# Graph network kernel: histogram products without the weights, weight sums by a segment scan, coefficient rows read ahead of four gather chunks

## The reference

```python
# layer 0: attention, one softmax per target over its edges
e = leaky_relu(concat([h[src], h[dst], emb_rel[etype]]) @ attn_w1 @ attn_w2, 0.01)
a = softmax of e over the edges of each dst
x = x + relu(where(deg > 0, segment_sum(a * h[src], dst), h) + h @ loop_weight)
# layer 1: plain sums over source nodes
x = x + relu(concat([h, segment_sum(h[dst] @ W_msg + b_msg, src)]) @ W_upd + b_upd)
# layer 2: two rounds with edge weights w
norm = maximum(segment_sum(w, dst), 1.0) ** -0.5
h = segment_sum((h * norm)[src] * w, dst) * norm        # twice; mean of the three h
# layer 3: attention with 8 heads and self loops, then a two-layer net with layer norms
```

## Time and profile before

| what | us |
|---|---|
| runs | 3965.01, 3946.61, 3963.30 (median 3963.3) |
| the profiled execution | 3954.3 |
| its span, first to last instruction | 3952.6 |
| PE busy | 2834.4 |
| VectorE busy | 2382.7 |
| POOL busy | 1904.0 |
| ScalarE busy | 480.0 |
| mean granted clock | 0.64 |

### The profile page before, as it was taken

The page is one execution under the profiler, slowest core; times in us unless marked ns, Lnnn a source line. Parts: engine busy times, 40 slices in busy tenths (PEclk is TensorE's granted clock), DMA queues, the critical chain, the costliest instruction groups (busy, mean ns, idle before and its releaser), DMA issues.

```text
span 3952.6 us, 46035 instructions
## 1 busy us (share of the span) xinstructions
PE 2834.4 (72%) x14097; PEld 2257.3 (57%) x14098; DVE 2382.7 (60%) x4263; ACT 480.0 (12%) x934; POOL 1904.0 (48%) x1767
## 2 busy tenths in 40 slices
PE   1984688788888499979979947777300226999894
PEld 1981111577777399979923336666300006999873
DVE  5678999777777688830010069999708463555433
ACT  0000000233323000014400012222100011000011
POOL 1778777767777200000000047777078787777200
PEclk9555555555555555559989969999755555555575
DMA  2314455387887622205466801111021134244100
GB/s 88 122 48 103 110 141 144 96 191 184 198 183 185 175 78 81 62 17 183 157 259 255 296 27 50 52 52 51 35 67 42 53 124 134 84 117 118 32 1 8
DMA packets 244087, 434.92 MB, mean 110 GB/s; under 512 B 137949, under 2 KB 139847, under 8 KB 230391
## 3 DMA queue, kind: packets, MB, share of 16 engines
q10 hardware_dynamic: 126289, 182.23, 16.6%
q1 hardware_dynamic: 60614, 190.34, 13.1%
q0 software_dynamic: 57056, 60.74, 8.3%
HBM read 276.41 MB, written 156.60 MB: 110 GB/s over the span
## 4 chain that ended last, share of the span: by engine, by line
PE 50%; DVE 18%; POOL 13%; issue 10%; DMA 6%; DVEq 1%; ACT 1%; ACTq 1%; SPq 0%; POOLq 0%
POOL ring L620 10%; PE PS L975 9%; PE PS L1180 7%; PE PS L1080 6%; PE PS L1082 5%; PE PS L1013 4%; PE PS L1151 4%; PE PS L1215 3%; DVE big L1921 3%; DMA qa<-d_code 3%; DMA arena<-d_code 2%; PE PS L1262 2%; PE PS L1159 2%; PE PS L1205 2%; DVE big L1915 2%
## 5 line engine op out<-in xcount | busy, mean ns | idle before, releaser
L620 POOL DMA_INDIRECT ring<-d_h,idx_lin x1568 | 1675.3, 1068 | 1581.7 <-DMA d_h<-Hn 1038.4
L1080 PE MATMUL PS<-qa 128*125 128x150 bf16 x1050 | 414.4, 395 | 105.8 <-DVE arena L1654 46.1
L1262 PEld LDWEIGHTS PS<-arena,s_ring 128*128 128x128 f32 x1968 | 438.4, 331 | 9.8 <-issue 1.3
L1262 PE MATMUL PS<-arena,s_ring 128*128 x1968 | 432.4, 414 | 0.0
L1082 PE MATMUL PS<-qa 128*125 128x150 bf16 x1050 | 401.1, 382 | 0.0
L975 PEld LDWEIGHTS PS<-arena,s_ring 128*125 128x125 f32 x1632 | 342.8, 332 | 0.4 <-issue 0.4
L975 PE MATMUL PS<-arena,s_ring 128*125 x1632 | 342.8, 416 | 0.0
L1080 PEld LDWEIGHTS PS<-qa 128*125 128x125 bf16 x1050 | 262.6, 250 | 135.9 <-DVE qa L1647 95.9
L1847 DVE TENSOR_SCALAR s_ring<-iota_row,arena 128x125 f32<-128x125 f32 x816 | 280.4, 346 | 77.7 <-ACT arena L719 19.8
L1180 PE MATMUL PS<-big,arena 125*64 125x500 f32 (+1 forms) x700 | 268.7, 546 | 25.7 <-DVEq L1315 25.7
L1082 PEld LDWEIGHTS PS<-qa 128*125 128x125 bf16 x1050 | 264.3, 252 | 0.0
(11 more groups left out here) (441 smaller groups left out, 4068.0 us busy)
## 6 DMA issues: line engine op xcount, KB each, us to landing
big<-d_wgt SPq DMA_DIRECT2D x50, 1562.5 KB, 7.4
d_stash<-ring SPq DMA_DIRECT2D x196, 256.0 KB
arena<-d_stash ACTq DMA_DIRECT2D x196, 256.0 KB, 2.7
big<-d_cnt SPq DMA_DIRECT2D x25, 1562.5 KB, 6.5
ring<-d_h,idx_lin POOLq DMA_INDIRECT x1568
d_cnt<-big ACTq DMA_DIRECT2D x13, 1562.5 KB
d_wgt<-big ACTq DMA_DIRECT2D x13, 1562.5 KB
d_cnt<-arena ACTq DMA_DIRECT2D x12, 1562.5 KB
```

Of the source, the lines that this page charges most:

```text
L620: pool.indirect_dma_start(ring[:, HALF * h + s, :], None, table, bass.IndirectOffsetOnAxis(ap=idx_lin[:, CH * i + s:CH * i + s + 1], axis= ...
L1080: nc.tensor.matmul(bank(3 * half + s // 2, NP, 2 * CW, at), lhs, hot_step(half, s, W, 2 * CW), start=(s % 2 == 0), stop=False, skip_group_ ...
L1262: mm = nc.tensor.matmul(PS[:, bass.ds(place[s] + j % SUMS * BANK, D)], marks[:, j % 2, s, :], arena[:, bass.ds(at[s], D)], start=False, st ...
```

## The change

- The histogram multiplies the counts' one-hot alone: the moving operand has 25 columns instead of 100. L1447, `w3` with its five preparing instructions, and the reduction into `norm` (L1474) go.
- The edge weights are written to memory (`d_wl`) beside the other edge tables, and read back to `w_edge` before the softmax ends. Behind `softmax0`, VectorE clears `norm` and runs one `scan_one` over them, which gives a running sum per target (`w_sum`); PE gets one more `chain` for it. SP writes it to `d_wsum`, and POOL reads the sum at each target's last edge into `norm` with 25 indirect transfers.
- SP's stash loop stops before chunk 94 (`ALPHA_AT`): there it issues the load of `w_edge`, waits for the coefficients and writes them. POOL stops before the same chunk, waits for that write, reads the coefficient rows and only then gathers chunks 94 to 97. `d_wsum` and the first count blocks follow on SP behind the rest of the stash loop.
- Wait counts of later semaphore uses are raised accordingly.

```diff
-        h_bf = s_flat[:, RING * W // 2:RING * W // 2 + RING * 4 * HW // 2].bitcast(BF16)
+        h_bf = s_flat[:, RING * W // 2:RING * W // 2 + RING * HW // 2].bitcast(BF16)
...
@@ sync
             sp.dma_start(d_dst.rearrange("(p c) k -> p (c k)", p=P), junk[:, 0:C]).then_inc(S["dst_out"], 16)
+            sp.dma_start(d_wl.rearrange("(p c) k -> p (c k)", p=P), w_lin).then_inc(S["dense_out"], 16)
...
                         sp.dma_start(fa0, d_fa0.rearrange("(p c) k -> p (c k)", p=P)).then_inc(S["fill_in"], 16)
+                    if turn == 0 and i == ALPHA_AT:
+                        sp.wait_ge(S["blk_ready"], NB)
+                        sp.wait_ge(S["dense_out"], 32)
+                        sp.wait_ge(S["fill_in"], 16)
+                        sp.dma_start(w_edge, d_wl.rearrange("(p c) k -> p (c k)", p=P)).then_inc(S["fill_in"], 16)
+                        sp.wait_ge(S["alpha_ready"], 1)
+                        sp.dma_start(d_al0.rearrange("(p c) k -> p (c k)", p=P), qa[:, 0:C]).then_inc(S["alpha_out"], 16)
                     sp.wait_ge(S[f"stash_got{h}"], CH * 16 * stash_turns(turn, i))
...
             stash(0)
 
-            sp.wait_ge(S["alpha_ready"], 1)
-            sp.dma_start(d_al0.rearrange("(p c) k -> p (c k)", p=P), qa[:, 0:C]).then_inc(S["alpha_out"], 16)
-
             sp.wait_ge(S["blk_out0"], 32 * (NB // 2 + 2))
             sp.wait_ge(S["blk_out1"], 32 * (NB // 2 + 1))
             sp.wait_ge(S["alpha_out"], 16)
+            sp.wait_ge(S["alpha_ready"], 2)
+            sp.dma_start(d_wsum.rearrange("(p c) k -> p (c k)", p=P), w_sum).then_inc(S["alpha_out"], 16)
             sp.wait_ge(S["steps_in"], 32)
...
@@ gpsimd
             block_rows(d_dst, dstl, "drow0_in")
-            tiles(0, d_h0, 40, NCH)
+            tiles(0, d_h0, 40, ALPHA_AT)
             pool.wait_ge(S["alpha_out"], 16)
             block_rows(d_al0, alpha0, "rows_in")
+            tiles(0, d_h0, ALPHA_AT, NCH)
...
+            pool.wait_ge(S["alpha_out"], 32)
+            for b in range(NB):
+                pool.indirect_dma_start(norm[:, b:b + 1], None, d_wsum, bass.IndirectOffsetOnAxis(ap=last_i[:, b:b + 1], axis=0),
+                                        bounds_check=EP - 1, oob_is_err=False).then_inc(S["nodes_in"], 16)
...
@@ tensor
-                mm = nc.tensor.matmul(bank(7, NP, 4 * NB), free(s_bf[:, 0:1], [[HALF, NP]], h * W * HALF + s_),
-                                      free(h_bf[:, 0:1], [[HW * HALF, 4], [HALF, NB]], h * 4 * HW * HALF + s_),
+                mm = nc.tensor.matmul(bank(7, NP, NB), free(s_bf[:, 0:1], [[HALF, NP]], h * W * HALF + s_),
+                                      free(h_bf[:, 0:1], [[HALF, NB]], h * HW * HALF + s_),
                                       start=(c == 0), stop=(c == C - 1))
...
             chain(1)
             chain(1, 1)
+            chain(1)
             pe.wait_ge(S["rows_in"], 16 * KG)
...
@@ vector
-            for j in range(3):
-                go(v_.tensor_copy(w3[:, j, :], w_lin))
-                if j < 2:
-                    go(v_.tensor_tensor(w_lin, w_lin, w3[:, j, :], ALU.subtract))
...
-                go(v_.tensor_tensor(hot_d, iota_d[:, 0:HW, :], dhi_at[:, :, c:c + HALF], ALU.is_equal))
-                v_.tensor_tensor(free(h_bf[:, 0:1], [[HW * HALF, 3], [HALF, HW], [1, HALF]], (h * 4 + 1) * HW * HALF),
-                                 free(h_bf[:, 0:1], [[0, 3], [HALF, HW], [1, HALF]], h * 4 * HW * HALF),
-                                 w_at[:, :, :, c:c + HALF], ALU.mult).then_inc(S["hist_s"], 1)
+                v_.tensor_tensor(hot_d, iota_d[:, 0:HW, :], dhi_at[:, :, c:c + HALF], ALU.is_equal).then_inc(S["hist_s"], 1)
...
             go(v_.tensor_copy(deg[:], hist[:, 0:NB]))
-            go(v_.tensor_reduce(norm[:], hist[:, NB:4 * NB].rearrange("p (k b) -> p b k", b=NB), AX_X, ALU.add))
...
             softmax0()
+            v.wait_ge(S["fill_in"], 32)
+            go(v_.memset(norm[:], 0.0))
+            scan_one(w_edge, w_sum, notst, cf_sum, SUMOP, 0.0)
+            mark("alpha_ready")
             v.wait_ge(S["rows_sb"], R_SB)
...
             go(v_.tensor_scalar(Hn[:], Hn[:], 0.0, None, ALU.max))
+            v.wait_ge(S["nodes_in"], 16 * NB)
             go(v_.tensor_scalar(st[:, 1, :], norm[:], 1.0, None, ALU.max))
```

More of the change, by code:

```diff
@@ L132, in gnn_four_layers @@
         d_dst = dram("d_dst", (EP, 1))
+        d_wl, d_wsum = dram("d_wl", (EP, 1)), dram("d_wsum", (EP, 1))
         d_start = dram("d_start", (N, 1))
@@ L238, in gnn_four_layers @@
         zrow = qa[:, 0:C]
+        w_edge, w_sum = qa[:, C:2 * C], qa[:, 2 * C:3 * C]
         fa0 = qa[:, 9 * C - 16:10 * C - 16]
@@ L248, in gnn_four_layers @@
         HW = NB + 1
-        h_bf = s_flat[:, RING * W // 2:RING * W // 2 + RING * 4 * HW // 2].bitcast(BF16)
-        assert RING * W // 2 + RING * 4 * HW // 2 <= RING * P
+        h_bf = s_flat[:, RING * W // 2:RING * W // 2 + RING * HW // 2].bitcast(BF16)
+        assert RING * W // 2 + RING * HW // 2 <= RING * P
         lk = s_flat[:, 0:6 * LC // 2].bitcast(BF16).rearrange("p (q b m) -> p q b m", q=3, b=2)
@@ L255, in gnn_four_layers @@
         at = 12 * C
-        w3 = big[:, at:at + 3 * C // 2].bitcast(BF16).rearrange("p (j c) -> p j c", j=3)
-        at += 3 * C // 2
         iota_h = big[:, at:at + W * HALF // 2].bitcast(BF16)
@@ L446, in gnn_four_layers @@
         assert NCH % 2 == 0
+        ALPHA_AT = 94
         def of_part(i, c, m=1):
@@ L653, in _ @@
             pool.wait_ge(S["k5_ready"], 1)
-            pool.wait_ge(S["dense_out"], 16)
+            pool.wait_ge(S["dense_out"], 32)
             for g in range(DG):
@@ L687, in _ @@
             tiles(1, d_h3, 53, 59)
-            pool.wait_ge(S["alpha_out"], 16 * 2)
+            pool.wait_ge(S["alpha_out"], 16 * 3)
             alpha_rows = d_al3.rearrange("(t e) k -> t (e k)", e=P)
@@ L897, in _ @@
             act.dma_start(big[:, w3:2 * w3], d_fb3.rearrange("(p c) k -> p (c k)", p=P)).then_inc(S["fill_in"], 16)
-            act.wait_ge(S["alpha_ready"], 2)
+            act.wait_ge(S["alpha_ready"], 3)
             act.dma_start(d_al3.rearrange("(p c) k -> p (c k)", p=P), qa[:, 0:w3]).then_inc(S["alpha_out"], 16)
@@ L1438, in _ @@
             dhi_at = free(dhi_b[:, 0:1], [[0, HW], [1, C]])
-            w_at = free(w3[:, 0, 0:1], [[C, 3], [0, HW], [1, C]])
             iota_d = iota_h.rearrange("p (c s) -> p c s", s=HALF)
@@ L1471, in _ @@
             v.wait_ge(S["hist_used"], C + RING)
-            hist = bank(7, NP, 4 * NB)
+            hist = bank(7, NP, NB)
             go(v_.tensor_copy(deg[:], hist[:, 0:NB]))
-            go(v_.tensor_reduce(norm[:], hist[:, NB:4 * NB].rearrange("p (k b) -> p b k", b=NB), AX_X, ALU.add))
             mark("tri_in")
@@ L1492, in _ @@
             v.wait_ge(S["r5_tr"], 1)
-            v.wait_ge(S["dense_out"], 16)
+            v.wait_ge(S["dense_out"], 32)
             R5, firsti, lasti, t0, n5, one, off5 = tw(0), tw(1, True), tw(2, True), tw(3), tw(4), tw(5), tw(6)
@@ L1805, in softmax3 @@
                 mark("scan_ready")
-                v.wait_ge(S["nodes_in"], 16 * NB)
+                v.wait_ge(S["nodes_in"], 16 * NB * 2)
                 a_s, a_d = asd[:, :, 0:H], asd[:, :, H:2 * H]
@@ L1815, in softmax3 @@
                 mark("fill_ready")
-                v.wait_ge(S["fill_in"], 16 * 2)
+                v.wait_ge(S["fill_in"], 16 * 3)
                 fbuf = big[:, 0:2 * w]
@@ L1828, in softmax3 @@
                 mark("scan_ready")
-                v.wait_ge(S["nodes_in"], 16 * NB * 2)
+                v.wait_ge(S["nodes_in"], 16 * NB * 3)
                 pack_b = packed(nfill, nh)
@@ L1836, in softmax3 @@
                 self_part()
-                v.wait_ge(S["fill_in"], 16 * 3)
+                v.wait_ge(S["fill_in"], 16 * 4)
                 scan_all(fb, fb, nh, notst, cf_sum, SUMOP, 0.0)
```

2 lines of the change are left out of this document (1 added, 1 removed).

## The result

The changed kernel takes 3947.09 us (median of 20 runs, 3932.5 to 3956.0), the kernel before, run beside it, 3954.62 (20 runs, 3943.1 to 3972.1). The ratio is 0.9976, 95% interval [0.9964, 0.9987]: 9.5 us less, between 5 and 14. The forecast was 3947.8, with -9.5 as its sum. (The 9.5 us are the ratio's; the two medians lie 7.5 us apart.) It is a gain that can be told from zero only by many runs, and inside the 0.5% that the forecast called no change.

A forecast was written before the change was run, and what follows sets the result against it. No engine is busy throughout, so it followed the chain of waits, with PE bounding the histogram. Terms -3.8 - 0.5 - 0.25 + 0 (histogram) - 4.9 = -9.5 us, from 3957.3 to 3947.8; range 3895 to 3966.

The forecast's parts named there:

- The histogram's step: Histogram products on PE: the load is last, so the step stays at 229 ns; 0 us, with -15 for the range.
- VectorE's wait "near 0.9 us instead of 0.45" a group: Histogram, sign of being right: VectorE waits longer for PE before each group of eight columns.
- the last coefficient row lands in under 3 us: Coefficient row reads before layer 0, sign of being right: the last landing falls from 7.27 us to under 3.
- L1447 in the last group and L1474: Histogram's end on VectorE: only the last group's share of L1447 counts, -0.50 us, and L1474 gives -0.25.
- The weight parts: Before the first layer norm on VectorE: three casts and two subtractions leave the chain, -3.8 us.
- The last landing: Coefficient reads before layer 0: without count blocks beside them the last lands in 2.4 instead of 7.27 us, -4.9 us.
- The scan and the chain for the weight sums: Behind the softmax, VectorE and PE: added work hidden by 11 us until the rows are in, 0; uncovered it costs 5.6 us.
- POOL: Before and in layer 0: POOL idles until the coefficients are written, then its 65 transfers, 81 us, cost the chain 0.
- The slower rival: Layer 0's steps: POOL's transfers hold VectorE's masks, at the full 0.94 us each costing 42 us, time 3990; chance 0.03.
- SERIES: Histogram: load and stream add up, so fewer moving columns shorten the step, 49 us, time 3899; chance 0.21.
- the 74 us by the load rule: Histogram: an estimate with a load of 104 ns whatever the stride gives a step of 135 ns, 74 us gained.
- The reads land as late as before: Coefficient reads before layer 0: they queue on themselves, not behind the blocks; sum -4.6, time 3952.7, inside the forecast's own range.

The follow-up runs named there:

- cols100: The changed kernel with 100 moving columns in the histogram again, its 25 one-hot columns read four times over: 3945.99 us, ratio 0.9974 to the kernel before.
- inter4: The changed kernel with the histogram's stationary one-hots interleaved by 4 columns instead of 8: 3884.73 us, ratio 0.9825 to the kernel before.
- w3_back: The changed kernel with the three casts and two subtractions of the weight parts put back ahead of the first layer norm: 3950.29 us in one run.
- rows_behind: The changed kernel with coefficient rows read behind the whole gather and coefficients written behind the whole stash loop: 3950.64 us, ratio 0.9981 to the kernel before.
- scan4: The changed kernel with the scan of the weights and PE's chain for it done four times instead of once: 3953.68 us, ratio 0.9998 to the kernel before.
- blocks_first: The changed kernel with the first three count blocks loaded right behind the coefficients' write, ahead of the last stash writes: 3950.62 us, ratio 0.9998 to the kernel before.
- inter4_behind: inter4 with coefficient rows read behind the whole gather and coefficients written behind the whole stash loop: 3947.66 us, ratio 0.995 to the kernel before.
- inter4_early: inter4 with the coefficient rows read ahead of the last twelve gather chunks instead of the last four: 3885.93 us, ratio 0.9802 to the kernel before.
- swap4: The changed kernel with the histogram product's operands exchanged and the moving one-hots interleaved by 4: 3906.7 us, ratio 0.9855 to the kernel before.

## Why the prediction was right, point by point

- **The histogram's step** (0, with -15 kept): 229.7 to 228.9 ns, -0.6 us. `cols100` shows that the moving columns don't count here, `inter4` that the load's spacing does. The -15 us kept for a load that gains when less streams beside it did not come. The reading that carried this was the distance from a load's start to its own matmul, taken as the time of the stream (0.16 us at 100 columns). It holds in three kernels: 0.158 us at 100 columns, 0.046 at 25, 0.222 at 125 (medians of the records), 1.6 to 1.8 ns a column each time. With 25 columns it looks like this (timelines, changed kernel):

```profile
129.63 0.84 PE L1026 MATMUL PS<-s_ring 128*125 128x25 bf16 x3
```

```profile
129.81 0.55 PEld L1026 LDWEIGHTS PS<-s_ring 128*125 128x125 bf16 x2
```

  The load is put down 0.18 us behind the matmul ahead, although the load is what is last; so a load's recorded start is not where its work begins, and a record of 0.325 us can't be laid into a step of 0.229.
- **VectorE's wait "near 0.9 us instead of 0.45" a group** was a slip: the earlier trace rows give 62.2/96 = 0.65, and with the 0.48 of L1447 the sum is 1.13. Measured: 111.4/96 = 1.16. The forecast did not rest on it. The sign "the last coefficient row lands in under 3 us" missed as well, by 0.07.
- **L1447 in the last group and L1474** (-0.75): with the step's -0.6 the table's second line should read -1.35; it reads -1.4.
- **The weight parts** (-3.8): the five take 3.8 us in `w3_back`, of which 3.4 reach the first product; the table has -4.0 there. The first layer norm stands 3.8 us earlier (its subtraction begins at 69.25 instead of 73.03).
- **The last landing** (-4.9): the mechanism was right, the term too large. An undisturbed last row takes 3.04 to 3.09 us in the kernels where nothing collides, not the 2.4 that I took as the shortest of the earlier trace rows. So -4.2; one of the seven reads took 1.42 us to issue, which left -3.7 in this trace. The place of the reads gave nothing, as the prediction said ("they would also be on time"), and `rows_behind` confirms it.
- **The scan and the chain for the weight sums** (0, with 11 us of cover): hidden, with 10 us between PE's last transpose and the rows; `scan4`.
- **POOL** (waits for the coefficients anyway; its 65 transfers don't hold VectorE): 85 us idle, passes unchanged with 140 transfers. A single-column read takes POOL 1.27 us, not the 0.94 that all 65 were given, so this work lasts some 8 us longer than forecast, still hidden. The slower rival is refuted, with its hold measured at 0.29 us at most.
- **The rivals.** SERIES was given 0.21 and falls with `cols100`; the 74 us by the load rule of the Trainium skill's TensorE: Matmul & The Clock Gate (LDWEIGHTS (loading the stationary operand)) fall with it, as its 104 ns don't hold at 16 bytes. "The reads land as late as before" falls with `blocks_first`.
- **The sum** of what was measured at its places is -4.0 - 1.4 - 3.7 = -9.1; the runs give -9.5, between -5 and -14. That they agree better than that interval is luck, and so is the time itself, 3947.8 against 3947.09: the forecast started from 3957.3 for the kernel before, which ran at 3954.6 in the comparison.

## What to carry to other kernels

Before the moving side of a product is trimmed, ask whether load or stream is last: a step costs the longer of the two, and each costs by the spacing of its operand in memory as well as by its columns. Where operands are interleaved so that VectorE writes whole runs, halve the interleave once: from 8 to 4 elements it cost VectorE nothing and PE's step fell from 0.229 to 0.117 us, from 4 to 2 VectorE lost more than PE gained (stage 115 us instead of 101). And a placement that is worth nothing today (the rows read ahead of four chunks) can be what most of a later gain hangs on: some 60 of 69 us, by the ratios of `inter4_behind`, `inter4_early` and the changed kernel. Look at the idle time of the engine that is passed, and leave it more than the spread between traces.

## What was not expected of the hardware

- The spacing sets the price of a moving column and of a stationary one alike, and not the clock: 16 bytes 1.83 (stationary) and 1.78 ns (moving), 8 bytes 0.92 to 0.94; the dense blocks' 150 moving columns at 12 bytes take 0.21 us, 1.40 ns each, on the same line. In `swap4` the granted clock was at its upper level for all but the first 39 of the 784 products, and the step stayed at 0.115 us:

```profile
120.00:190.00 70.00, 68.63 (x548) 55.64 (x545) 58.71 (x139) 0.00 (x0) 54.45 (x52) 1.00 0.20 47
```

  (a window of 70 us; the changed kernel stands at 0.50 there). What raised the clock in this kernel alone isn't settled: the node products ahead of the histogram are the same, and PE was busy 4.53 of the 4.60 us before it rose, but it is as busy in the others.
- The dense blocks' 2100 products read both operands at 12 bytes, and by this rule a shorter spacing would shorten their steps. It wasn't tried. VectorE would write shorter runs there, and it is busy 404 of 540 us in that stage, with PE waiting for it.
- The first chip of the experiments and the last differ by 0.4% for the same kernel (3953.9 and 3969.2 us), with the dense stage 557 us long on one and 563 to 569 on the other. Ratios can be compared between chips, times can't.
